# One-core macaron block: down weights and last tile apart, late operands on VectorE, one expert's weights through memory

## The reference

```
x = x + 0.5 * ffn(layernorm(x))
x = x + attention(layernorm(x))      # 16 heads of 16, causal
x = x + 0.5 * ffn(layernorm(x))      # the same weights again
```

## Time and profile before

| | us |
|---|---|
| median of three runs | 744.22 |
| the profiled execution's own time | 745.51 |
| its span, first to last instruction | 743.6 |
| PE busy in the span | 731.7 |
| DVE busy | 471.7 |
| POOL busy | 416.6 |
| ACT busy | 348.7 |

### The profile page before, as it was taken

One profiled execution on the slowest core, in us unless ns is written; L12 is line 12 of the kernel. 1 busy time (PEld: TensorE's weight loads), 2 busy tenths in 40 slices (PEclk: granted clock), 3 DMA queues, 4 the chain that ended last, 5 costly groups with the idle time before them and its releaser, 6 DMA issues.

```text
span 743.6 us, 13761 instructions
## 1 busy us (share of the span) xinstructions
PE 731.7 (98%) x4712; PEld 587.6 (79%) x4712; DVE 471.7 (63%) x1307; ACT 348.7 (47%) x663; POOL 416.6 (56%) x497
## 2 busy tenths in 40 slices
PE   7999999999999989999999999999999999999998
PEld 6888889877778767777777778777777778888887
DVE  5978855866566747778557757964658533563333
ACT  5456346254465534656445456454364552422322
POOL 2687484554663525844555853463554665646663
PEclk9999999999999999999999999999999999999999
DMA  8455224734233633324652423654322233223331
GB/s 284 161 181 176 84 92 123 191 113 139 76 106 115 170 104 96 112 92 130 173 151 57 136 83 108 161 138 146 118 70 97 87 111 110 85 73 130 112 101 56
DMA packets 69717, 90.20 MB, mean 121 GB/s; under 512 B 13200, under 2 KB 49424, under 8 KB 69648
## 3 DMA queue, kind: packets, MB, share of 16 engines
q1 hardware_dynamic: 67184, 88.75, 38.9%
q10 hardware_dynamic: 2464, 0.58, 0.4%
HBM read 72.10 MB, written 17.04 MB: 120 GB/s over the span
## 4 chain that ended last, share of the span: by engine, by line
PE 83%; DMA 4%; SPq 3%; DVE 2%; POOL 1%; issue 1%; ACT 1%; ACTq 0%; POOLq 0%; DVEq 0%
PE ra L814 14%; PE ra L816 13%; PE ra L815 13%; PE dn L836 7%; PE dn L837 7%; PE dn L838 7%; PE ra L935 4%; PE ra L919 4%; PE ra L947 4%; SPq L1519 2%; PE ra L775 2%; PE ra L895 1%; PE ra L908 1%; PE ra L897 1%; PE ra L896 1%; PE ra L910 1%
## 5 line engine op out<-in xcount | busy, mean ns | idle before, releaser
L1437 POOL TENSOR_TENSOR hid<-hid,wb 128x512 f32<-128x512 f32 x124 | 162.4, 1312 | 171.2 <-DVE hid L1291 160.4
L814 PE MATMUL ra<-xt_hi,wgu_hi 128*128 128x512 f32 x508 | 219.3, 432 | 0.1
L1441 POOL TENSOR_TENSOR ht_lo<-hid,ht_hi 128x512 fp32r<-128x512 f32 x124 | 162.3, 1311 | 98.8 <-ACT ht_hi L1057 98.6
L816 PE MATMUL ra<-xt_lo,wgu_hi 128*128 128x512 f32 x508 | 200.6, 395 | 0.0
L815 PE MATMUL ra<-xt_hi,wgu_lo 128*128 128x512 f32 x508 | 200.4, 394 | 0.0
L836 PE MATMUL dn<-wd,ht_hi 128*128 128x256 f32 x512 | 163.0, 318 | 0.7 <-POOL ht_lo L1441 0.7
L1283 DVE SCALAR_TENSOR_TENSOR hid<-hid,ra 128x512 f32<-128x512 f32 x125 | 85.6, 684 | 115.3 <-ACT hid L1049 114.5
L1343 DVE CUSTOM_DVE_ANT_0 junk<-ra,mask 128x128 bf16<-128x128 f32 (+3 forms) x256 | 115.1, 485 | 64.9 <-PE ra L919 62.8
L837 PE MATMUL dn<-wd,ht_hi 128*128 128x256 f32 x512 | 143.6, 281 | 0.0
L838 PE MATMUL dn<-wd,ht_lo 128*128 128x256 f32 x512 | 143.5, 280 | 0.0
L1057 ACT ACTIVATE ht_hi<-hid 128x512 fp32r<-128x512 f32 x124 | 78.0, 629 | 138.4 <-POOL hid L1437 111.0
(11 more groups left out here) (170 smaller groups left out, 807.6 us busy)
## 6 DMA issues: line engine op xcount, KB each, us to landing
wd<-wd_parts SPq DMA_DIRECT2D x56, 512.0 KB, 3.9
wb<-wts_rows SPq DMA_DIRECT2D x62, 256.0 KB, 3.9
qk_parts<-parts SPq DMA_DIRECT2D x32, 192.0 KB, 2.2
q_st<-qk_parts SPq DMA_DIRECT2D x96, 64.0 KB, 2.6
k_st<-qk_parts SPq DMA_DIRECT2D x96, 64.0 KB, 2.4
wd_parts<-wd SPq DMA_DIRECT2D x8, 512.0 KB, 3.8
ctx_rows<-cx SPq DMA_DIRECT2D x16, 256.0 KB, 2.7
stage<-in_Wg SPq DMA_DIRECT2D x8, 256.0 KB, 4.4
```

Of the source, the lines that this page charges most:

```text
L814: mm(b_, w_hi, xt_hi[q % 2][:, c, :], start=c == 0, stop=False)
L816: last = mm(b_, w_hi, xt_lo[q % 2][:, c, :], start=False, stop=c == KT - 1)
L1437: nc.gpsimd.tensor_tensor(tb, tb, wb[m % NWB][:, :], ALU.mult).then_inc(hw_done, 1)
L1441: nc.gpsimd.tensor_tensor(ht_lo[n % NHT][:, :], hidden(n)[:, :], f32(ht_hi[n % NHT][:, :]), ALU.subtract).then_inc(lo_done, 1)
```

## The change

Six edits. Four change instructions or semaphores (the third of them also the path of one expert's weights); the late operands and the due times change the order alone:

- **Start.** WARM is 13 in place of 16. ACT rounds expert 0's gate and up weights in one instruction in place of two.
- **Down weights apart.** Wd has its own semaphore; `sg` waits for Wg and Wu alone.
- **Second expert's first weights.** NWP = 1: `wbp` is made for expert 0 alone, expert 1's tile is loaded from memory like all later ones.
- **Late operands.** For DVE, the planner counts `rec` as ready 1.5 us and `nm` 1.0 us later than its model of the transfers says.
- **Last tile apart.** In the last block the fourth token tile gathers in a bank of its own, taken from `ra`; DVE adds tiles 2 and 3 in two instructions, and SP stores them in two transfers.
- **Due times.** Attention, the down products of the first chunks, expert weights and the norm of several blocks get other due times.

```diff
-WARM = 16
+WARM = 13
+NWP = 1
-Q1 = 8.0
-DOWN0, DOWN1 = 3.6, 0.87
-M0, PERIOD = 27.6, 4.5
+Q1 = 8.36
+DOWN0, DOWN1 = 3.45, 0.86
+M0, PERIOD = 27.78, 4.44
@@ schedule()
-        sg = (-9.46, -8.8, 0.4, 3.3, 5.2, 7.6, 9.3, 11.0)[e]
-        sd = (-8.85, 0.9)[e] if e < NWD else down[FT * (e - NWD) + FT - 1] + 0.42
+        sg = (-9.46, -8.8, 0.67, 3.18, 5.47, 7.6, 9.16, 11.24)[e]
+        sd = (-8.85, 0.25)[e] if e < NWD else down[FT * (e - NWD) + FT - 1] + 0.42
-    put(1.62, ("wbp", 1))
-        start = CB * (q - 1) + {1: Q1, 2: 3.0, 4: 2.2, 5: 7.5, 6: 6.8, 7: 8.2}.get(q, 5.0)
+        start = CB * (q - 1) + {1: Q1, 2: 3.40, 4: 1.52, 5: 7.5, 6: 6.93, 7: 8.21}.get(q, 5.0)
-        if m >= NWB:
+        if m >= NWP:
-        head = meet[0] - (9.8 if b else 8.65)
+        head = meet[0] - (9.86 if b else 8.78)
+LATE = {"rec": 1.5, "nm": 1.0}
@@ Plan.run(), earliest()
-            t = max(free[e], ready[key] + (0.0 if e != "pe" ...
+            t = max(free[e], ready[key] + (LATE.get(o["item"][0], 0.0) if e == "dve" else 0.0) + (0.0 if e != "pe" ...
@@ plan()
-            add("act", ("sg", 0), 0.55, ("sp", "ld", 0))
-            add("act", ("sgx",), 0.55, ("sp", "ld", 0), then=[("act", "xt", 0, 1)])
+            add("act", ("sg", 0), 1.0, ("sp", "ld", 0))
-            add("dve", ("sgx",), 0.62, ("act", "sgx"), port=True, then=[("dve", "xt", 0, 1)])
+            add("dve", ("sgx",), 0.62, ("act", "sg", 0), port=True, then=[("dve", "xt", 0, 1)])
+            add("pe", ("d", n, i), 0.355, *([("pool", "lo", n)] + ready if i == 0 else []),
+                takes=("last",) if n == NCH - CB and i == QT - 1 else None)
@@ PE, "d"
+                        apart = q == NBLOCK - 1 and i == QT - 1
+                        if apart and k == 0 and TURN["last",] > 0:
+                            pe.wait_ge(ra_free[BANK["last",]], TURN["last",])
-                        if k == CB - 1 and i == 1:
+                        if k == CB - 1 and (i == 1 or i == 2 and q == NBLOCK - 1):
                             last.then_inc(half_done, 1)
@@ ACT, "sg" and "sd"
-                        act.wait_ge(stage_in[e % NSTAGE], 48 * (e // NSTAGE + 1))
+                        act.wait_ge(stage_in[e % NSTAGE], 32 * (e // NSTAGE + 1))
...
+                        act.wait_ge(stage_d_in[e % NSTAGE], 16 * (e // NSTAGE + 1))
@@ DVE, "add"
-                        for m in range(2):
+                        for m in range(2 if q < NBLOCK - 1 else 1):
...
+                        if q == NBLOCK - 1:
+                            for i, sums_of in ((2, dn[1]), (3, rbank(("last",)))):
+                                dve.wait_ge(*((half_done, q + 2) if i == 2 else (down_done, CB * (q + 1))))
+                                xt = x_res[:, b * QT + i, :]
+                                nc.vector.tensor_tensor(xt, sums_of[:, 0:D], xt, ALU.add).then_inc(x_done, 1)
@@ POOL, "hi"
-                        if m < NWB:
+                        if m < NWP:
                             pool.wait_ge(*emptied(("wbp", m)))
@@ SP
-                    if kind == "wb" and it[1] >= NWB:
+                    if kind == "wb" and it[1] >= NWP:
-                        sp.wait_ge(hw_done, FT * (m - NWB + 1))
+                        if m >= NWB:
+                            sp.wait_ge(hw_done, FT * (m - NWB + 1))
+                        for k, (i, size) in enumerate(((0, 2), (2, 2)) if q < NBLOCK - 1 else ((0, 2), (2, 1), (3, 1))):
+                            sp.wait_ge(x_done, 2 * q + k + 1)
```

More of the change, by code:

```diff
@@ L169, in schedule @@
     for m in range(NBLOCK * E):
-        if m >= NWB:
-            put(max(high[FT * (m - NWB) + FT - 1] + 0.45, wt_at[m // E] + 0.35), ("wb", m))
+        if m >= NWP:
+            put(max(high[FT * (m - NWB) + FT - 1] + 0.45 if m >= NWB else 0.0, wt_at[m // E] + 0.35), ("wb", m))
         if m >= E:
@@ L274, in earliest @@
             e = o["eng"]
-            t = max(free[e], ready[key] + (0.0 if e != "pe" or o["item"][1:2] == (0,) else MARGIN.get(o["item"][0], 0.0)))
+            t = max(free[e], ready[key] + (LATE.get(o["item"][0], 0.0) if e == "dve" else 0.0) + (0.0 if e != "pe" or o["item"][1:2] == (0,) else MARGIN.get(o["item"][0], 0.0)))
             if o["port"]:
@@ L410, in plan @@
         add("dve", ("h", n), 0.6, ("dve", "t", n), ("pe", "u", n, 1), frees=("u", n))
-        add("pool", ("hi", n), 1.25, ("dve", "h", n), ("sp", "wb", m) if m >= NWB else ("act", "wbp", m), port=True)
+        add("pool", ("hi", n), 1.25, ("dve", "h", n), ("sp", "wb", m) if m >= NWP else ("act", "wbp", m), port=True)
         add("act", ("hi", n), 0.53, ("pool", "hi", n), ("pe", "d", n - NHT, QT - 1) if n >= NHT else None)
@@ L422, in plan @@
         for i in range(QT):
-            add("pe", ("d", n, i), 0.355, *([("pool", "lo", n)] + ready if i == 0 else []))
+            add("pe", ("d", n, i), 0.355, *([("pool", "lo", n)] + ready if i == 0 else []),
+                takes=("last",) if n == NCH - CB and i == QT - 1 else None)
     for q in range(NBLOCK):
@@ L427, in plan @@
             add("sp", ("add", q), 0.9, ("dve", "add", q))
-    for m in range(NWB, NBLOCK * E):
+    for m in range(NWP, NBLOCK * E):
         store = ("act", "wt", 0) if m < E else ("sp", "wt", m // E)
-        add("sp", ("wb", m), 0.4, store, ("pool", "hi", FT * (m - NWB) + FT - 1), kb=256)
+        add("sp", ("wb", m), 0.4, store, ("pool", "hi", FT * (m - NWB) + FT - 1) if m >= NWB else None, kb=256)
     for m in range(E, NBLOCK * E):
@@ L483, in plan @@
             add("sp", ("wt", q), 0.4, ("act", "wt", q), kb=16)
-    for m in range(NWB):
+    for m in range(NWP):
         add("pe", ("wbp", m), 0.95, ("dve", "route", 0, ROUTE_PIECES - 1))
@@ L672, in build @@
         stage_in = [sem(f"stage_in{i}") for i in range(NSTAGE)]
+        stage_d_in = [sem(f"stage_d_in{i}") for i in range(NSTAGE)]
         consts = sem("consts")
@@ L833, in _ @@
                         w_hi, w_lo = wd[m % NWD][:, f, 0:D], wd[m % NWD][:, f, D:2 * D]
-                        b_ = dn[i // 2][:, i % 2 * D:(i % 2 + 1) * D]
+                        apart = q == NBLOCK - 1 and i == QT - 1
+                        if apart and k == 0 and TURN["last",] > 0:
+                            pe.wait_ge(ra_free[BANK["last",]], TURN["last",])
+                        b_ = rbank(("last",))[:, 0:D] if apart else dn[i // 2][:, i % 2 * D:(i % 2 + 1) * D]
                         h_hi, h_lo = (h[n % NHT][:, i * P:(i + 1) * P] for h in (ht_hi, ht_lo))
-                        mm(b_, h_hi, w_hi, start=k == 0 and i % 2 == 0, stop=False, skip_group_check=True)
+                        mm(b_, h_hi, w_hi, start=k == 0 and (i % 2 == 0 or apart), stop=False, skip_group_check=True)
                         mm(b_, h_hi, w_lo, start=False, stop=False, skip_group_check=True)
@@ L979, in _ @@
                         e = it[1]
[L980 to L988 removed]
+                        act.wait_ge(stage_in[e % NSTAGE], 32 * (e // NSTAGE + 1))
+                        nc.scalar.activation(wgu_hi[:, e, :, :], stage[e % NSTAGE][:, :, 0:2 * F],
                                              ACT.Copy).then_inc(g_hi, 1)
@@ L1220, in _ @@
                         else:
[L1221 removed]
+                            dve.wait_ge(g_hi, e + 1)
                             nc.vector.tensor_tensor(wgu_lo[:, e, :, :], stage[e % NSTAGE][:, :, 0:2 * F],
@@ L1419, in _ @@
                         e = it[1]
-                        pool.wait_ge(g_hi, e + 2)
+                        pool.wait_ge(g_hi, e + 1)
                         nc.gpsimd.tensor_tensor(wgu_lo[:, e, :, :], stage[e % NSTAGE][:, :, 0:2 * F],
@@ L1468, in _ @@
                             sp.dma_start(stage[i][:, :, w * D:(w + 1) * D],
-                                         A[name][e].rearrange("(k p) f -> p k f", p=P)).then_inc(stage_in[i], 16)
+                                         A[name][e].rearrange("(k p) f -> p k f", p=P)
+                                         ).then_inc(stage_d_in[i] if name == "Wd" else stage_in[i], 16)
                     if kind == "la":
@@ L1552, in _ @@
                         b = q % BATCH
-                        for m in range(2):
-                            sp.wait_ge(x_done, 2 * q + m + 1)
-                            sp.dma_start(out[b * T + m * HT:b * T + (m + 1) * HT, :].rearrange("(i p) d -> p i d", p=P),
-                                         x_res[:, b * QT + 2 * m:b * QT + 2 * m + 2, :]).then_inc(out_sem, 16)
-                sp.wait_ge(out_sem, 32 * BATCH)
+                        for k, (i, size) in enumerate(((0, 2), (2, 2)) if q < NBLOCK - 1 else ((0, 2), (2, 1), (3, 1))):
+                            sp.wait_ge(x_done, 2 * q + k + 1)
+                            rows = out[b * T + i * P:b * T + (i + size) * P, :].rearrange("(i p) d -> p i d", p=P)
+                            sp.dma_start(rows, x_res[:, b * QT + i:b * QT + i + size, :]).then_inc(out_sem, 16)
+                sp.wait_ge(out_sem, 32 * BATCH + 16)
 def kernel(**inputs):
```

18 lines of the change are left out of this document (4 added, 14 removed).

## The result

The changed kernel took 738.37 us (737.57 to 739.09, 6 runs), the kernel before on the same chip 744.25 us (743.82 to 746.02, 6 runs). The ratio is 0.9911, 95% between 0.9900 and 0.9923. The sign was right, the size too small: 6.6 us came where I had summed 4.93. That the sum is not further off is luck: its largest term was priced too high, and the terms that I had put at nothing too low.

What follows compares the result with a forecast made beforehand. The prediction took PE, busy 731.7 of 743.6 us, as the bound. Its terms, 3.88 + 0.8 + 0.1 + 0.15 = 4.93 us, taken from the 744.22 us median, gave 739.3 us, range 738.0 to 743.6.

Steps and rivals of the forecast that it cites:

- What bounds the kernel: Over the whole kernel: PE is the bound, busy 731.7 of 743.6 us; gains come from its work, waits, start and end.
- Late operands, 3.88: Near 270 us: `mt` ahead of `rec` removes PE's 2.18 us `q_st` wait and the 1.70 us clock loss; 3.88 us.
- Due times and the waits not yet counted: Over the rest of the order: PE's remaining waits are drawn anew; taken as 0, bounds -3.9 and +1.0 us.
- Second expert's first weights, 0.8: Near 24 us: eight fewer broadcast records and an earlier free bank save PE 1.17 us, of which 0.8 survives.
- Start, 0.1: Before the first gate product: with three fewer warm products the second transposes start slightly earlier; 0.1 us, bounds -0.3 and +0.6.
- Down weights apart elsewhere, 0: ACT's later roundings, after the start: they begin before DVE can use them, so no gain; 0.
- Last tile, 0.15: At the end: the smaller last store saves 0.25 us, its issue comes 0.1 later; 0.15 us gain, bounds -0.2 and +0.6.
- C: Rival: one large PE wait with the low clock remains or comes back; 743.2 us, no change; chance 0.14.
- D: Rival: late operands ahead of `mt` in two of the 16 groups, each costing 3.9 us; slower, 747.1 us; chance 0.11.
- E: Rival, at the start: the clock rises 2 us later, costing 1.0 us; 740.3 us; chance 0.05.

Runs made afterwards that it cites:

- before again: The kernel before, run and profiled a second time with no edit: 744.32 us, ratio 0.9996 to the kernel before.
- after again: The changed kernel, run and profiled a second time with no edit: 738.92 us, ratio 0.9918 to the kernel before.
- experiment 1: The kernel before with one `rec` put behind `mt` in DVE's order, nothing else moved: 743.92 us, ratio 0.9996.
- experiment 4: The kernel before with the late operands alone, order planned anew: 742.49 us, ratio 0.9975.
- experiment 3: The changed kernel without the late operands (LATE empty): 739.17 us, ratio 0.9933 to the kernel before.
- experiment 5: The kernel before with the late operands and all new due times, no edits to instructions or semaphores: 742.10 us, ratio 0.9972.
- experiment 9: The changed kernel with all due times of the kernel before, order planned anew: 743.18 us, ratio 0.9983 to the kernel before.
- experiment 7: The changed kernel with the second expert's broadcast made by PE again, order planned anew: 740.52 us, ratio 0.9939 to the kernel before.
- Experiment 8: The changed kernel, same order, with the gate and up rounding waiting for Wd too, as before: 739.77 us, ratio 0.9928 to the kernel before.
- experiments 10: The changed kernel with the two transfers of `k_st`'s constant rows moved behind tanh of chunk 2: 737.99 us, ratio 0.9904 to the kernel before.
- experiment 11: The changed kernel with the constant rows' transfers moved later and the last store issued from ACT's queue: 738.38 us, ratio 0.9919 to the kernel before.
- experiment 12: The changed kernel with the first expert's rounding in two halves again, order planned anew: 738.69 us, ratio 0.9923 to the kernel before.

## Why the prediction was right or wrong

One account for four executions, from their traces. A wait counts as the distance between the starts of two products, less the median distance of such a pair (the waits for `ct_lo`, whose pair is rare, by their idle time); so a wait can be longer here than its idle time in the lists. Work is what is left between first gate and last product.

| us | before | before again | after | after again |
|---|---|---|---|---|
| first gate product | 11.38 | 12.00 | 11.65 | 11.12 |
| PE waits before 100 us | 1.42 | 0.99 | 0.55 | 0.86 |
| PE waits after 100 us | 3.32 | 3.58 | 0.00 | 0.55 |
| of these for `q_st` | 2.17 | 0.71 | 0 | 0 |
| time lost to the low clock | 1.71 | 0 | 0 | 0 |
| work | 722.14 | 722.42 | 720.64 | 720.76 |
| last PE product | 739.97 | 738.99 | 732.84 | 733.29 |
| from it to the last landing | 3.25 | 3.27 | 3.26 | 3.25 |

Means of each pair: waits 4.66 to 0.98, 3.7 less; work 1.6 less, of which the broadcast is 0.9 and the other 0.7 was not taken apart; clock 0.9 less; start 0.3 less; end 0. Together 6.4, beside medians that differ by 6.6 and 6.1 (0.9911 and 0.9918 of 744). The early waits that are left are the one for the bank behind `wt`, 0.55 and 0.53, where both traces of before have 0.36, and 0.33 at 96.8 us in the second.

*What bounds the kernel.* Right. PE was the bound and still is, and most of the gain came out of its waits and its work.

*Late operands, 3.88.* The mechanism of the one wait stands: `rec` at the head of DVE's queue kept `mt` back, and with `mt` first that wait is gone (experiment 1). The size fails. The profiled execution of before was a dear one: `q_st` cost 2.17 and the clock 1.71 there, 0.71 and nothing in the next. The swap alone gives 0.04%, within its interval, and the late operands alone 0.25%, with a wait of 0.97 for `q_st` left at 241.54 us (experiment 4). And in the change as made, it isn't they that remove it: without them the wait is gone as well (experiment 3). I had taken one execution's single largest wait, with its clock, as what every run pays; and I subtracted the 1.29 by which that execution was above the median from the level, but not from the term that had made it dear.

*Due times and the waits not yet counted, "I take 0".* This is the step that failed, and it outweighs the other. In before the waits after 100 us other than for `q_st` are 1.15 in one execution and 2.87 in the other; in after they are 0 and 0.55. With the early waits they come to 3.2 us in the mean against 0.98, 2.2 less, of which my sum had 0.28. My upper bound of +1.0 read the list of PE's waits by its two largest rows and counted the rest as tenths. The old due times in the new kernel cost 4.8 to 5.4 us (0.9983 less 0.9918 or 0.9911, of 744): the term that I had priced at nothing decides whether the rest of the change is worth anything. It has no value of its own, though: on the old structure the same due times add nothing that can be told to the late operands (experiment 5 beside 4).

*The parts need each other.* My sum added the parts as if each had a price of its own. All with the late operands: neither new due times nor new structure gives 0.25%, the due times without the structure 0.28%, the structure with the old due times 0.17%, both together 0.8 to 0.9%. In the traces this shows as waits, counted as in the table: 3.5 us in experiment 4, 1.9 us in experiment 5, all of it early, 5.9 us in experiment 9 (at `mx`, `probs`, `rest` and the first broadcast above all), and 0.5 and 1.4 in the two traces of after. The new due times suit the new structure, and the old ones don't. What makes a given due time right was not tried one by one. Of the 4.0 to 4.5 us that the structure adds to the new order, experiments 7 and 8 find 1.6 and 0.85 (unclear); the rest is open.

*Second expert's first weights, 0.8.* Direction right, size half: 1.6 us by experiment 7, 0.89 of work and the rest, as its trace suggests, early waits. Two details were wrong: the bank isn't free at 23.5, and the trip through memory ends 2.9 us later than before, not 0.8 to 1.7. For the first, the wait behind `wt` that was to go grew by 0.2; behind the second no product of PE waited.

*Start, 0.1.* In the profiled pair it is 0.27 the wrong way. Over more traces it is a little better than I said: the first gate product starts at 11.82 in the mean of five kernels with the old start (11.38 to 12.24) and at 11.45 in the mean of seven with 13 warm products (11.03 to 11.96), 0.4 sooner, with a scatter as large. Much of that scatter goes with the time at which the rate of the warm products rises: in the seven, from 11.03 with a rise at 8.3 to 11.96 with a rise at 10.4. The reading that ACT's queue, not the landing of Wd, held the first rounding was right, but freeing it brought nothing that can be told (experiments 10 and 11). Rounding in one or two makes no difference (experiment 12).

*Down weights apart elsewhere, 0.* Open. Experiment 8 leans to 0.85, with a wait of 0.8 for POOL near 94 us, and doesn't decide it.

*Last tile, 0.15.* Measured 0. The durations were right (0.41 for an add, 0.25 saved by the smaller transfer); the step that failed is the last issue, 0.25 later and not 0.1. The Trainium skill, DMA: Bandwidth & Descriptors, section Anatomy of one DMA, would have given 0.30 for the bytes of 128 KB; the traces show 0.25 less for a store of 128 KB than for one of 256 KB, and 0.2 of it lost again in experiment 11, where the third store is issued closer behind and from the other queue.

*Rivals.* C and D, another `q_st` wait with the low clock, did not come in the traces of kernels with the new due times, nor a mean clock below 0.999 in 44 executions of those that have the new structure too. E happened: the rate rose at 9.4 and not at 8.0 in the profiled execution. There it was hidden behind `xn`; over the seven traces a rise 2.1 us later goes with a first gate product 0.9 later, close to the 1.0 for 2 us by which I had priced it.

## What to carry to other kernels

Before a stall of one trace is priced, take a second execution of the same kernel, or look at the list of mean clocks and times of all runs: a stall that depends on a transfer's time is no constant, and its largest showing is what catches the eye. On an engine that is 98% busy, add up all its waits, not the two largest; a new order that has none can be worth their sum. When a trace shows an early first product, look at when the clock rose in it before the edit gets the credit. After an edit that moves work between engines, plan the order anew before judging the edit: here neither was worth more than 0.3% without the other, and both together 0.8 to 0.9%.

## What the hardware showed that I had not expected

- On one chip, executions of the kernel before spread over 5.4 us (26 runs) and those with the swap over 4.5 (12), but those with the late operands over 2.7 (12), with the new due times too over 1.6 (9), and those of the changed kernel without late operands over 2.1 (6). `den` made DVE idle for 4.42 us in one execution and 3.06 in another of the same kernel; that this is what spreads the times is not shown.
- An idle time of 2.01 us was followed by 3.41 us at 1.2 GHz, one of 0.55 us at the same place by none.
- The rise of the clock at the start, read from where PE's records go from 0.21 to 0.11 us apart, came anywhere from 7.1 to 10.4 us in the 14 traces, with warm products running from 4.1 to 4.4 us in all of them. At 10.4 (experiment 9) all 13 warm products had been made at the low clock, the last of them before 9.95.
- However the last stores are cut here and whichever queue issues the last, it lands 3.25 to 3.27 us after PE's last product, in the four traces of the table and in that of experiment 11.
